# The skip term D·u of a state-space decoder layer: from diagonal matmuls on TensorE to one VectorE instruction for each channel block

## The reference, cut to what matters

```python
# mixer: u is silu(conv(x_in)), (b, 1024 channels, 512 tokens)
delta = softplus(dt_proj(dt) + dt_proj_bias)
def step(h, inputs):                       # over 512 tokens
    d_t, B_t, C_t, u_t = inputs
    h = h * exp(d_t[..., None] * A) + (d_t * u_t)[..., None] * B_t[:, None, :]
    return h, einsum('bdn,bn->bd', h, C_t) # 16 states n, summed
y = ys + u * D                             # D: 1024 values
y = y * silu(z)
out = out_proj(y)
# experts: 16 logits for each token, two experts each, and 4 shared blocks
routing = softmax(x3 @ gate_w.T); topw, sel = top_k(routing, 2)
shared = sigmoid(x3 @ shared_gate_w.T) * (silu(x3 @ ws_gate.T) * (x3 @ ws_up.T) @ ws_down.T)
```

## Time and profile before

| what | before |
|---|---|
| three runs, us | 1648.68, 1650.03, 1644.61 |
| profiled execution: its time, its span, us | 1648.9, 1647.2 |
| mean granted TensorE clock | 0.939 of full speed |
| TensorE busy (share of the span) | 1411.3 us (86%) |
| VectorE busy | 1327.2 us (81%) |
| GpSimd busy | 1033.4 us (63%) |
| ScalarE busy | 802.4 us (49%) |

### The profile page before, as it was taken

The page is one execution under the profiler, slowest core; times in us unless marked ns, Lnnn a source line. Parts: engine busy times, 40 slices in busy tenths (PEclk is TensorE's granted clock), DMA queues, the critical chain, the costliest instruction groups (busy, mean ns, idle before and its releaser), DMA issues.

```text
span 1647.2 us, 19279 instructions
## 1 busy us (share of the span) xinstructions
PE 1411.3 (86%) x5382; PEld 809.1 (49%) x5382; DVE 1327.2 (81%) x2196; ACT 802.4 (49%) x1369; POOL 1033.4 (63%) x672
## 2 busy tenths in 40 slices
PE   7588679998799999999699999989699999746994
PEld 4333234444465665444465665444456664334783
DVE  4588999687999999787999999797899999784212
ACT  3675454247544665246544665246644664131131
POOL 0299899104899898403899898403999898422001
PEclk9799889999799999999799999999799999968997
DMA  3550000413446673614447673614446673601884
GB/s 121 225 192 26 1 0 16 157 45 141 162 154 223 198 237 105 217 43 162 166 147 218 204 241 103 219 45 161 166 147 182 216 244 100 249 26 42 350 333 138
DMA packets 94073, 252.13 MB, mean 153 GB/s; under 512 B 11024, under 2 KB 11152, under 8 KB 88848
## 3 DMA queue, kind: packets, MB, share of 16 engines
q1 hardware_dynamic: 86688, 229.93, 41.1%
q0 software_dynamic: 5120, 16.78, 3.0%
q10 hardware_dynamic: 2160, 4.19, 0.8%
HBM read 207.87 MB, written 42.99 MB: 152 GB/s over the span
## 4 chain that ended last, share of the span: by engine, by line
PE 47%; DVE 22%; issue 12%; POOL 10%; ACT 5%; DMA 2%; DVEq 0%; SPq 0%; POOLq 0%; ACTq 0%
PE bank L2014 10%; DVE bank L1328 5%; POOL work L691 5%; PE bank L1854 5%; PE bank L2140 5%; PE bank L1944 4%; PE bank L1949 4%; PE bank L2043 4%; PE bank L1938 3%; PE bank L1867 2%; PE bank L2035 2%; PE bank L1990 2%; DVE pairs L1338 2%; DVE work L1338 1%; DVE rr L1512 1%
## 5 line engine op out<-in xcount | busy, mean ns | idle before, releaser
L691 POOL TENSOR_TENSOR work<-du,BB 128x1024 f32<-128x1024 f32 x255 | 601.1, 2366 | 4.5 <-DVE work L1599 3.5
L983 ACT ACTIVATE bank<-delta,A_sb 128x512 f32<-128x512 f32 x512 | 349.0, 690 | 437.9 <-DVE pairs L1338 237.5
L1328 DVE TENSOR_TENSOR_SCAN bank<-bank,work 128x512 f32<-128x512 f32 x432 | 522.3, 1221 | 13.7 <-POOL work L691 7.4
L2014 PEld LDWEIGHTS bank<-x3T,ew_up 128*128 128x128 f32 x1488 | 218.6, 195 | 74.5 <-issue 65.7
L2014 PE MATMUL bank<-x3T,ew_up 128*128 128x128 f32 (+1 forms) x1488 | 239.1, 306 | 2.2 <-issue 2.2
L1338 DVE TENSOR_TENSOR pairs<-bank,CB 128x512 f32<-128x512 f32 x240 | 161.9, 675 | 4.3 <-PE bank L1949 2.9
L1944 PE MATMUL bank<-pairs,ident 128*128 128x512 f32 x160 | 90.7, 651 | 44.8 <-POOL pairs L744 17.5
L1338 DVE TENSOR_TENSOR work<-bank,CB 128x512 f32<-128x512 f32 x192 | 129.1, 672 | 0.0
L643 POOL TENSOR_TENSOR col<-col,halfpow 128x4 f32<-128x4 f32 (+1 forms) x8 | 7.3, 912 | 178.6 <-DVE col L1476 178.6
L2140 PE MATMUL bank<-wst,zg 128*128 128x512 f32 x256 | 117.0, 593 | 0.8 <-DVE zg L1348 0.8
L1867 PE MATMUL bank<-xT,wst 128*128 128x512 f32 x256 | 116.2, 599 | 0.0
(11 more groups left out here) (263 smaller groups left out, 2364.9 us busy)
## 6 DMA issues: line engine op xcount, KB each, us to landing
ew_up<-in_exp_w SPq DMA_DIRECT2D x93, 512.0 KB, 3.7
ew_dn<-in_exp_w SPq DMA_DIRECT2D x93, 256.0 KB, 4.4
hm<-xs_dram SPq DMA_DIRECT2D x69, 256.0 KB, 4.6
ys_dram<-x3T SPq DMA_DIRECT2D x69, 256.0 KB, 4.6
wst<-in_w_in SPq DMA_DIRECT2D x64, 256.0 KB, 2.6
BB<-bc_dram SPq DMA_DIRECT2D x16, 1024.0 KB, 6.3
CB<-bc_dram SPq DMA_DIRECT2D x16, 1024.0 KB, 7.0
wst<-in_out_w SPq DMA_DIRECT2D x32, 256.0 KB, 2.7
```

The lines of the kernel that those rows point to most:

```text
L691: nc.gpsimd.tensor_tensor(dBu[:, k % CHUNK_SLOTS, :, :], du[:, j % 2:j % 2 + 1, :].broadcast_to([P, 2, T]), BB[:, n0:n0 + 2, :], ALU.mult) ...
L983: nc.scalar.activation(R[q % RING][:, :], delta[:, j, :], ACT.Exp, scale=A_sb[:, j, n:n + 1]).then_inc(S["da_ready"], 1)
L1328: V.tensor_tensor_scan(prod[c % (2 * PAIR_SLOTS)] if on_pool(q) else R[q % RING][:, :], R[q % RING][:, :], dBu[:, c // 2 % CHUNK_SLOTS, c ...
L2014: ins = mm(gu_bank(v)[:, part * n:(part + 1) * n], w[:, part * D + k * P:part * D + (k + 1) * P], rhs, start=(k == 0), stop=(k == KD - 1))
```

## The change

1. **Skip term.** The diagonals (ScalarE) and their matmuls (TensorE) are gone. VectorE adds D·u to the finished sums in place, Y = u·D + Y (`skip`), at the position where it gated before; the gate comes one position later.
2. **x3T.** `sp_w` of blocks 4 to 7 lies in rows 12 to 15 of BB. ScalarE's copy into x3T goes to position 0 and no longer waits for the softplus sums. In exchange the broadcast that fills BB rows 12 to 15 waits for these sums, and is issued behind the first expert loads.
3. **Chunks.** GpSimd's four sums and four subtractions of softplus blocks 4 to 7 come one chunk later (behind chunk 3 and 4, not 2 and 3).
4. **Router.** Logits are formed as 128 tokens x 17 by 16 short matmuls straight into the place where VectorE reads them; copy and transposes are gone. Router and first visits sit at earlier positions.

```diff
-STAGE = Order(visits=tuple(6 + 15 * v // 4 for v in range(SHARED)) + tuple(38 + 3 * r for r in range(ROUTED)),
-              x3=3, logits=4, logits_copy=5, route=7, rank=11, place=12, first_down=14)
+STAGE = Order(visits=tuple(4 + 4 * v for v in range(SHARED)) + tuple(38 + 3 * r for r in range(ROUTED)),
+              x3=0, logits=1, route=5, rank=9, place=10, first_down=12)
...
-                return late_pairs[:, m, :] if m < 4 else x3T[:, m - 4, :]
+                    return late_pairs[:, m, :] if m < 4 else BB[:, 8 + m, :]
...
-                if b > 0 and g == 3 and half == 1:
-                    sp.wait_ge(S["delta_ready"], NBLK * (b + 1))
+                if b > 0 and g == 3:
+                    sp.wait_ge(S["delta_ready" if half == 1 else "sum_ready"], NBLK * (b + 1))
...
-                        if k == 2 and b > 0:
+                        if k == 3 and b > 0:
                             for i in range(4, 8):
                                 softplus_sum(b, i)
-                        if k == 3 and b > 0:
+                        if k == 4 and b > 0:
                             for i in range(4, 8):
                                 softplus_less(b, i)
...
+                def skip(j):
+
+                    ve.wait_ge(S["nsum_done"], PAIRS * b + NS // 2 * (j + 1))
+                    V.scalar_tensor_tensor(out=Y[:, :], in0=u[:, j, :], scalar=dsk[:, j:j + 1], in1=Y[:, :],
+                                           op0=ALU.mult, op1=ALU.add).then_inc(S["skip_ready"], 1)
+
                 def gated(j):
 
-                    ve.wait_ge(S["nsum_done"], PAIRS * b + NS // 2 * (j + 1))
+                    ve.wait_ge(S["skip_ready"], NBLK * b + j + 1)
...
                     if scan and p >= NS + Y_BEHIND and p % NS == Y_BEHIND:
+                        skip(p // NS - 1)
+                    if scan and p >= NS + Y_BEHIND and p % NS == Y_BEHIND + 1:
                         gated(p // NS - 1)
...
-                        if m % (NS // 2) == NS // 2 - 1:
-                            j = m // (NS // 2)
-                            pe.wait_ge(S["skip_ready"], NBLK * b + j + 1)
-                            mm(Y[:, :], skip_diag(b, j), u[:, j, :], start=False, stop=False)
...
-                        ins = mm(bank[0][0:NE + 1, :], gatew[:, f, :], x3T[:, f, :], start=(f == 0), stop=(f == KD - 1))
-                    ins.then_inc(S["lgT_ps"], 1)
-                    pe.wait_ge(S["lgT_ready"], b)
-                    for t in range(TT):
-                        ins = nc.tensor.transpose(lg[:, t, :], lgT[:, t * P:(t + 1) * P], ident[0:NE + 1, 0:NE + 1])
+                        for t in range(TT):
+                            ins = mm(lg[:, t, :], x3T[:, f, t * P:(t + 1) * P], gatew[:, f, :],
+                                     start=(f == 0 and t == 0), stop=(f == KD - 1 and t == TT - 1))
```

41 lines of the change are left out of this document (5 added, 36 removed).

## The result

The changed kernel takes **1657.33 us** (median of 7 runs, 1654.18 to 1662.21); the kernel before, on the same chip, 1647.91 us (7 runs). The ratio is 1.0058, with a 95% interval of 1.0039 to 1.0077. The 19 runs of both have a median of 1655.9 us. So the change makes the kernel slower by 0.3 to 0.6%, some 5 to 9 us, where 1645.6 us was forecast, with a range up to 1656.

What follows compares the result with a forecast made beforehand. No single engine bounds it: mid-stage TensorE and VectorE wait for each other, at the end TensorE alone is late. Terms -3.75 + 1.9 - 1.2 = -3.05 us from 1648.9 gave 1645.8, as median 1645.6; range 1637 to 1656.

Steps and rivals of the forecast that it cites:

- What a skip costs on either side: Each of 32 skips gives TensorE 0.86 us back (27.5 in all) and costs VectorE 0.65 (20.8 in all).
- Blocks 0 and 1: In each stage with experts: two skips +1.3 us, against waits for gate, chunks and tanh that go; waits together -1.9.
- Blocks 2 to 5: In each stage with experts: four skips +2.6 us, gate waits shrinking by 2.05, together +0.55.
- The tail: End of each stage with experts: TensorE is the bound, so the skips of blocks 6 and 7 save 1.7 us.
- Batch 0: Scan without experts, TensorE waiting for VectorE: later gate +1.9, skips -0.86 and +2.6, tail -1.7; sum +1.9 us.
- rival B: Stages with scans: gate waits do not shrink because TensorE starves for the later gate; +9.5, 1658.2 us; chance 0.22.
- rival C: TensorE pauses more, one more low-clock stretch in each stage with experts; 5.6 us more, 1651.2 us; chance 0.16.
- Late stage: Last stage, router as the path: short logits take 3.4 us instead of 4.6, so -1.2 us, between 0 and -2.3.
- Start of the scan stages: Stages with experts: third chunk and sums clash with softplus, first scan 4.8 us late; +1.8 once routing is done.
- 3.0 us "regained": Start of stages with experts: vanished waits of 1.5 us for a chunk, 1.0 for router transposes, 0.5 at line 1774.
- Blocks and tail of stages 1 to 3: Batches 1 to 3: start, blocks and tail together -1.25 us in each stage, three of them -3.75.

Runs made afterwards that it cites:

- b_no_du: The kernel before with D·u left out altogether (no diagonals, no matmuls, no VectorE instruction): 1639.44 us, ratio 0.9941.
- b_skip: The kernel before with D·u alone moved to VectorE and the gate one position later: 1656.80 us, ratio 1.0046.
- a_b0_diag: The changed kernel with D·u of batch 0 alone back on TensorE: 1652.42 us, ratio 1.0018.
- b_b0_skip: The kernel before with D·u on VectorE in batch 0 alone, the gate there one position later: 1653.84 us, ratio 1.0024.
- b_skip_together: The kernel before with D·u on VectorE and the gate right behind it, at its old position: 1657.39 us, ratio 1.0056.
- the first pair: The changed kernel, 1657.33 us, and the changed kernel with the wide (uncut) router in the last stage, 1652.59 us.
- a_b0_late: The changed kernel with D·u of batch 0 on TensorE and the wide router in the last stage: 1650.95 us, ratio 1.0007.
- after_again: The changed kernel itself, measured a second time: 1654.94 us, ratio 1.0030 to the kernel before.
- late_wide_again: The changed kernel with the wide router in the last stage, measured a second time: 1653.59 us, ratio 1.0014.
- c_short: c_diag with the short router in the last stage too, as in the changed kernel: 1646.02 us, ratio 0.9985.
- c_diag: The changed kernel with D·u on TensorE everywhere, the old chunk order and the wide router in the last stage: 1644.74 us, ratio 0.9966.
- a_no_skip: The changed kernel with D·u back on TensorE and the gate at its old place: 1648.07 us, ratio 0.9986.
- a_no_skip_late: The changed kernel with D·u back on TensorE and the wide router in the last stage: 1648.19 us, ratio 0.9994.
- c_wide: c_diag with the wide router in all stages, leaving only early x3T and the earlier router and visit positions: 1642.28 us, ratio 0.9951.
- a_chunk2: The changed kernel with GpSimd's softplus sums and subtractions one chunk earlier again, as before: 1653.60 us, ratio 1.0026.
- c_b0: c_diag with D·u on VectorE in batches 1 to 3: 1647.81 us, ratio 0.9990.
- b_chunks: The kernel before with the change's order of GpSimd's chunks, sums and subtractions alone: 1660.56 us, ratio 1.0069.

## Why the prediction was wrong

**Where the forecast failed.** The failing step is "What a skip costs on either side" as it was carried into "Blocks 0 and 1", "Blocks 2 to 5", "The tail" and "Batch 0". The price of a single skip was right (0.74 us, 0.65 from start to start). Wrong was what the time is worth on each engine: waits that "go" were set off against new work on VectorE, and the tail was given back whole, as if both engines had the same room. b_no_du and b_skip measure it: TensorE's 27.5 us are worth 9.6, VectorE's 20.8 cost 17.4, a net of +7.8 us (b_skip alone: +7.3). In the prediction the terms of the skip alone are +1.3 - 1.4 + 2.6 - 2.05 - 1.7 = -1.25 in each of three stages and +1.9 in batch 0, together -1.85. (The other 1.8 us of "Blocks 0 and 1" are waits for chunks and the tanh.) These 9 us are most of the miss.

**Batch 0**, predicted +1.9, measured +5.5 (243.2 to 248.7 us in the two traces, 243.4 again in a_b0_diag, 248.1 in b_b0_skip). I had the tail begin 1.9 + 2.6 - 0.86 = 3.6 us later. Relative to the first scan it begins 5.1 later (255.20 - 69.05 against 259.95 - 68.70). The 1.9 for the gate's place is right: b_skip and b_skip_together differ by 1.9 at the gate of block 5. The skips are not: they make 2.9 us there in b_skip_together, where I had 1.7. In 175 to 256 VectorE works 80.34 of 81 us, and 80.92 in the kernel before, so there is no room for them; between the gates of blocks 4 and 5 it is 27.0 us where it was 25.6. The tail's 1.7 us of saved matmuls did not come either: from the gate of block 5 to the last it is 58.2 us, and was 57.8. TensorE waits 28.5 us for gates in 175 to 262, where it waited 11.7, and then runs at the low clock. TensorE's waits for the gate over these 87 us (total us, times, longest), first in the changed kernel, then in the kernel before:

```profile
PE bank L1915 <- DVE zg L1316: 28.5, 4, 9.3
```

```profile
PE bank L1944 <- DVE zg L1348: 11.7, 4, 3.4
```

Over 255 to 270, with TensorE's first matmuls behind that gate, the granted clock is 0.66 in the changed kernel and 0.89 before, in this order:

```profile
255.00:270.00 15.00, 10.05 (x23) 4.67 (x24) 12.89 (x16) 5.48 (x9) 11.88 (x7) 0.66 0.00 1
```

```profile
255.00:270.00 15.00, 14.80 (x43) 7.13 (x44) 15.00 (x18) 7.96 (x14) 15.00 (x8) 0.89 0.01 2
```

This is the mechanism of rival B, in the one batch where I had not put its weight, and of rival C behind it. In stages 1 to 3 of the changed kernel no first sum of a block waits for a gate, so there rival B did not come; what the skips cost there is VectorE's own time.

**Late stage**, predicted -1.2, measured +4.4 in the two traces (9.90 to 14.31 us), +1.9 to +2.4 at an equal start. The 3.4 us for the logits were near the price of the higher level: 32 x 0.11 = 3.5. What failed is the clock, which I had left out of the price: the short form fell to the lower level or stayed there in all seven traces, so the logits took 5.2 to 6.85 us, and it left the visits behind it at that level. The medians give less and scatter: 4.7 for the first pair, 1.5 for a_b0_diag and a_b0_late, 1.4 for after_again and late_wide_again, 1.3 for c_short and c_diag (3.1 by the ratios), and nothing for a_no_skip and a_no_skip_late. I would carry on 1.4, with 0 to 3 as its bounds.

**Start of the scan stages**, predicted 4.3 to 5.4 us, taken 4.8: right in mechanism, and a little too much. The first scan is 4.1 us later from the first softplus instruction, with five stretched instructions: 2.05 us for the third chunk, then 1.07 and 0.94 for two that meet the sums. The Trainium skill, page "SBUF — State Buffer", section "Who interferes with whom", has GpSimd's reads of SBUF exclude a VectorE instruction with two SBUF inputs, or one in a two-port mode, for its whole length; the trace agrees again, with 2.74 us at 788.97 for an instruction with both inputs in SBUF, where it was 0.69. Of the 3.0 us "regained" the 1.5 for chunk 4 and the router's 1.0 are gone; the 0.5 is now 0.7. What was undervalued is early x3T: TensorE was given no lead from it. Its pause ahead of the logits, 7.57 us before, is 5.49 in the changed kernel, 2.35 in c_diag and 2.52 in c_wide, where the old chunk order lets the Ln and the copies come early; c_wide gains 6.9 us by the medians, 8 by the ratio. And the clash costs less than it lengthens the link: c_diag against a_no_skip_late says 3.5 us for three stages, a_chunk2 against the changed kernel 2.3.

**Blocks and tail of stages 1 to 3.** The skips wait no more in mid stage, as predicted. Last gate to last gate the profiled executions give -1.7, -4.1 and +0.3 us, together -5.5, where -3.75 was predicted. This looks like a hit, but it is luck: a sum of x3T's gain, the chunks' loss and the price of D u, none of which had its size. The medians of c_b0 and c_diag give D u +3.1 us over these stages and what follows, where its own terms made -3.75. Their links and stages together are equal in the two traces (1101.0 and 1100.6 us). The 2.1 us by which the two executions differ lie in the last stage, where c_b0's logits ran at the low clock (12.03 us to the first rank, c_diag's 9.90). Whether the place of D u brings that about or chance does is not shown.

**The sum.** By pairs of medians D u on VectorE costs 7.3 us (b_skip), of it 4 to 5 in batch 0; early x3T with the earlier positions brings 6.9 (c_wide); the short router costs 2.5 in stages 1 to 3 (c_diag less c_wide, where the two intervals overlap) and 0 to 4.7 in the last; the chunk order 2.3 (a_chunk2), 3.5 (c_diag) or 11 (b_chunks, where the copies into x3T wait for the late sums). 7.3 - 6.9 + 2.5 + 1.4 + 3.5 = 7.8 us, against 5.4 and 9.4 measured. Each of these terms has an uncertainty of 2 us or more, so that the sum fits is weak evidence; of the single parts, the price of D u and the gain of c_wide are the two that stand clear of the noise.

## What to carry to other kernels

Where two engines are busy for 93% of a stage, ask with an ablation what each one's microsecond is worth before moving work between them: here the same operation was worth a third of its time on TensorE and five sixths on VectorE, and leaving it out altogether was one run that said so. A change of four parts should be measured part by part, even if its sum seems neutral: one part (early copies of x3T, with the positions they allow) was worth 0.5%, and the three others ate it. And where an engine works 99% of a window, a wait that vanishes from it is not a gain but the room that new work has used up.

## What the runs showed of the hardware

- A product of 512 columns with a 17-column weight, cut into 16 matmuls that move 17 columns each, takes 32 records of 0.11 us at the higher clock level and of 0.21 at the lower (a_no_skip). Uncut it is 8 records of 0.43 and of 0.85. By these rates the cut form would take 3.5 us at the higher level, an estimate, where the uncut one takes 3.6. Begun at the lower level they take 7.0 and 5.7 (the changed kernel, late_wide_again), since the clock rises within the uncut form there and not within the cut one.
- In the last stage TensorE's clock fell during the short matmuls in each of the four traces in which they began at the higher level, with TensorE 1.60 of 1.60 us busy just before the fall (a_no_skip).
- Two executions of one kernel (the changed one and after_again) differ by up to 3 us in one stage (stage 2: 256.1 and 259.2). A few microseconds between two profiled executions are no evidence here; medians of 9 and 12 runs on one chip (c_diag, c_b0) told 3 us apart.
- The first scan starts at 68.6 to 69.7 us in 8 of the 20 traces and at 70.4 to 71.6 in the others. The changed kernel itself has both, 68.70 and 70.44 (after_again), so this moves the end of one execution by 2 us whatever the edit.
